# GpSimd forms W0's low part after VectorE's first one-hots, sums the bias on its own, and tile 1's registers are loaded earlier

## The reference

```python
h = jnp.maximum(_layernorm(x), 0.0)
# first layer: attention over the edges
h = nodes @ W + b_w                      # nodes is the h above; W is 512 x 512
s_dst, s_src = h @ a[:512], h @ a[512:]
e = leaky_relu(s_dst[dst] + s_src[src] + b_a, 0.2)
w = exp(e); alpha = w / segment_sum(w, dst)[dst]
out = segment_sum(alpha[:, None] * h[src], dst)
# x = x + out; then a second layer: gates over 4 experts, the best two taken,
# each two graph convolutions with 512 x 512 weights
```

## Time and profile before

| | us |
|---|---|
| median of 3 runs | 743.95 |
| the profiled execution | 743.08 |
| its span in the trace | 741.3 |
| TensorE busy | 720.8 (97%) |
| VectorE busy | 425.9 (57%) |
| ScalarE busy | 397.9 (54%) |
| GpSimd busy | 191.0 (26%) |

### The profile page before, as it was taken

The page is one execution under the profiler, slowest core; times in us unless marked ns, Lnnn a source line. Parts: engine busy times, 40 slices in busy tenths (PEclk is TensorE's granted clock), DMA queues, the critical chain, the costliest instruction groups (busy, mean ns, idle before and its releaser), DMA issues.

```text
span 741.3 us, 12237 instructions
## 1 busy us (share of the span) xinstructions
PE 720.8 (97%) x3671; PEld 586.5 (79%) x3671; DVE 425.9 (57%) x1053; ACT 397.9 (54%) x897; POOL 191.0 (26%) x207
## 2 busy tenths in 40 slices
PE   7899999999999999999999999999999999999994
PEld 5698977888888888777777777878888888888883
DVE  7989889999752538622722622657443544444441
ACT  8856678676643521511511511347677667767751
POOL 4300000000000101850200010045656555655511
PEclk9999999999999999999999999999999999999998
DMA  9100001111501247799699695379834994438950
GB/s 210 38 4 3 4 3 27 43 35 36 168 6 58 85 126 240 217 326 337 230 350 328 200 359 191 99 198 285 277 81 89 263 346 119 86 68 221 294 157 7
DMA packets 46445, 115.21 MB, mean 155 GB/s; under 512 B 8340, under 2 KB 8552, under 8 KB 46361
## 3 DMA queue, kind: packets, MB, share of 16 engines
q1 hardware_dynamic: 28581, 77.60, 32.5%
q0 software_dynamic: 9136, 19.65, 11.7%
q10 hardware_dynamic: 8644, 16.86, 7.0%
HBM read 64.89 MB, written 50.08 MB: 155 GB/s over the span
## 4 chain that ended last, share of the span: by engine, by line
PE 89%; DVE 6%; ACT 2%; issue 2%; DVEq 0%; POOL 0%; ACTq 0%; POOLq 0%
PE ps L1794 16%; PE ps L1795 16%; PE ps L1796 16%; PE ps L2223 7%; PE ps L2222 6%; PE ps L2090 3%; PE ps L2091 3%; PE ps L2023 3%; PE ps L2017 3%; PE ps L2018 3%; DVE onehot_g L1307 3%; PE ps L1882 2%; PE ps L2153 2%; PE ps L1961 1%; PE ps L1994 1%
## 5 line engine op out<-in xcount | busy, mean ns | idle before, releaser
L1121 ACT ACTIVATE agn<-ps,rec 32x128 f32<-32x128 f32 x336 | 120.9, 360 | 39.1 <-PE ps L2223 35.1
L1055 ACT ACTIVATE slots<-he_t 125x512 fp32r<-125x512 f32 x40 | 25.4, 635 | 150.9 <-DVE he_t L1592 144.5
L2223 PE MATMUL ps<-slots,CTs 125*128 x230 | 89.9, 391 | 0.0
L1592 DVE TENSOR_TENSOR he_t<-ps,b_b 125x512 f32<-125x512 f32 x40 | 27.5, 691 | 105.7 <-PE ps L1796 72.6
L734 POOL DMA_INDIRECT hrow<-t_d,piece_i x80 | 76.3, 954 | 25.7 <-issue 24.1
L2222 PE MATMUL ps<-slots,CTs 125*128 x207 | 80.7, 390 | 0.0
L1757 DVE TENSOR_TENSOR tm<-ps,b_b 128x512 f32<-128x512 f32 x23 | 15.9, 691 | 83.9 <-PE ps L1796 83.9
L1794 PE MATMUL ps<-W,agT_hi 128*125 128x512 f32 x160 | 63.5, 397 | 0.0
L1794 PE MATMUL ps<-W,h2T_hi 128*125 128x512 f32 x160 | 63.4, 396 | 0.0
L1796 PE MATMUL ps<-W,agT_lo 128*125 128x512 f32 x160 | 63.3, 396 | 0.0
L1795 PE MATMUL ps<-W,agT_hi 128*125 128x512 f32 x160 | 63.2, 395 | 0.0
(11 more groups left out here) (327 smaller groups left out, 1679.0 us busy)
## 6 DMA issues: line engine op xcount, KB each, us to landing
he_d<-slots SPq DMA_DIRECT2D x30, 448.0 KB
slots<-he_d SPq DMA_DIRECT2D x30, 448.0 KB
w_d<-slots SPq DMA_DIRECT2D x3, 4096.0 KB, 18.6
slots<-w_d SPq DMA_DIRECT2D x24, 512.0 KB, 21.8
t_d<-he_t SPq DMA_DIRECT2D x40, 224.0 KB
raw<-in_L_gnn_Wl ACTq DMA_DIRECT2D x4, 1024.0 KB, 8.0
raw<-in_L_gnn_Wr ACTq DMA_DIRECT2D x4, 1024.0 KB, 5.6
slots<-in_L_gnn_Wl ACTq DMA_DIRECT2D x4, 1024.0 KB, 10.3
```

The costliest lines, as they stand in the source:

```text
L1121: last = a.activation(agn[32 * r:32 * r + 32, q, :], ps[n, 3 + i % 2, 128 * r:128 * r + 128], ACT.Copy, scale=rec[n, i, 4:5])
L2223: last = mm(o, CTs[:, t, :], part(k, P, t * 1024 + D, P), start=False, stop=t == T - 1)
```

## The change

On GpSimd, the product of the bias with `a_sum` and its sum over the row are now made with tensor_tensor operations (a multiply, nine halvings, an add of `b_a`), around W0_hi; W0_lo waits in addition for the fifth `step_ready`, the last one-hot of VectorE's tile 0. On VectorE `bias_source` is gone, and the registers of tile 1 are loaded inside `sources()`, between the products and the wait for the last of them.

```diff
-            g.tensor_tensor(a_sum[:], a_b[0:P, 0, :], a_b[0:P, 1, :], ALU.add).then_inc(ab_ready.sem, 1)
+            link(g.tensor_tensor(a_sum[:], a_b[0:P, 0, :], a_b[0:P, 1, :], ALU.add))
+            link(g.tensor_tensor(a_sum[:], a_sum[:], bw_b[:], ALU.mult))
             pool.wait_ge(*w0_in(16))
             g.tensor_copy(W0_hi[:], W0_f[:]).then_inc(w0_hi_ready.sem, 1)
+            n = D // 2
+            while n > 0:
+                link(g.tensor_tensor(a_sum[:, 0:n], a_sum[:, 0:n], a_sum[:, n:2 * n], ALU.add))
+                n //= 2
+            g.tensor_tensor(s_add[:], a_sum[:, 0:1], ba_c[:], ALU.add).then_inc(ab_ready.sem, 1)
             pool.wait_ge(*w0_hi_ready(1))
+            pool.wait_ge(*step_ready(BW))
             g.tensor_tensor(W0_lo[:], W0_f[:], f32(W0_hi[:]), ALU.subtract).then_inc(w0_lo_ready.sem, 1)
...
             def sources():
                 source_vectors(1)
+                flags = batch_flags(1)
                 dve.wait_ge(*wa_f_ready(2 * KC))
                 link(v.tensor_copy(wa[:, :, 0:2], wa_f[:]))
                 v.tensor_tensor(wa[:, :, 2:4], wa_f[:], f32(wa[:, :, 0:2]), ALU.subtract).then_inc(wa_ready.sem, 1)
-
-            def bias_source():
-                dve.wait_ge(*ab_ready(1))
-                v.scalar_tensor_tensor(a_sum[:], bw_b[:], 1.0, a_sum[:], ALU.mult, ALU.mult,
-                                       accum_out=ab[:, 0:1]).then_inc(ab_ready.sem, 1)
-                dve.wait_ge(*ab_ready(2))
-                v.tensor_scalar(s_add[:], ab[:, 0:1], ba_c[:], None, ALU.add).then_inc(wa_ready.sem, 1)
+                return flags
...
-                more, before = batch_flags(b) if b > 0 else first_flags
+                more, before = (first_flags, *second_flags)[b] if b < 2 else batch_flags(b)
...
                 if b == 0:
-                    sources()
-                if b == 2:
-                    bias_source()
+                    second_flags.append(sources())
                 if b == T - 1:
...
-                    dve.wait_ge(*wa_ready(2))
+                    dve.wait_ge(*ab_ready(1))
```

More of the change, by code:

```diff
@@ L1361, in spread_out @@
                                 ).then_inc(sd_ready.sem, 1)
+            second_flags = []
             for b in range(T):
```

## The result

| | before | after |
|---|---|---|
| median of 9 runs, us | 744.10 | 747.93 |
| lowest and highest | 743.65 to 745.34 | 746.09 to 753.37 |
| profiled execution, its span | 743.08, 741.3 | 747.93, 746.2 |

The ratio is 1.0062, with a 95% interval of 1.0047 to 1.0077. Forecast were 744.1 us, no change, and a range up to 745.0: the measured median lies outside, on the slow side. The runs also lie further apart than before.

A forecast was written before the change was run, and what follows sets the result against it. TensorE, busy 97% of the span, was taken as the bound, so front delays pass through. +1.0 us at tile 1 and -0.81 at tile 3 gave +0.2 and 744.1 us, no change; range 741.4 to 745.0.

The forecast's parts named there:

- The mechanism: W0_lo enters after VectorE's first source product and holds the second some 4.4 us; TensorE waits for hT_lo and wa; chance 0.52.
- the first rival: VectorE's products run free beside W0_lo; -2.3 us, 741.65 us, faster; chance 0.26.
- the second rival: W0_lo gets in only at hT_lo or behind product 8; 743.55 or 744.7 us, no change; chance 0.12 for both forms.
- rival 3: Bias adds delay VectorE's first one-hots by 1.3 to 1.9 us, on top of the blocked products; 745.7 us, slower; chance 0.10.
- the two rules weighed: GpSimd blocked against VectorE's two-port modes only, or also operations with two SBUF inputs against a GpSimd operation reading SBUF.
- The step of tile 3: Without bias_source and its stall on VectorE, TensorE's tile-3 step falls from 7.61 to 6.80 us: -0.81 us.
- The sum: +1.0 us for TensorE late at tile 1, -0.81 at tile 3: +0.2 us.
- The prediction is wrong if the granted clock falls in TensorE's two new gaps: Stated sign of failure, without a size; the clock had stayed 1.00 from 20 to 33 us with 3 us idle.
- The start of tile 1: TensorE's tile 1 transposes start at 42.45 instead of 41.46 us: +1.0, bounds +0.7 to +1.9.
- The multiply was not hidden: Forecast that GpSimd's bias multiply, 1.27 us from 18.9 to 20.2, is hidden before W0_hi, which waits until 21.39.
- The scores behind a wait: TensorE's scores wait for wa until 41.65 and take 0.80 us before tile 1's transposes at 42.45.
- The moved loads: Some 1.2 of 1.6 us of VectorE's tile 1 register loads go; earns nothing itself, keeps the loss at 1.0.

The follow-up runs named there:

- E2: Changed kernel with W0_lo filled with zeros by a GpSimd memset in place of the subtraction: 740.72 us, ratio 0.9973 to the kernel before.
- E4: Changed kernel with W0_lo back directly behind W0_hi without its wait, the halvings and last add behind it: 741.96 us, ratio 0.9992 to the kernel before.
- E3: Kernel before with only W0_lo's added wait for the fifth step_ready: 745.5 us, ratio 1.0046.
- E11: Changed kernel with only the bias multiply moved behind W0_hi: 746.41 us, ratio 1.0028 to the kernel before.
- E1: Changed kernel with 15 filler matmuls before TensorE's wait for hT_lo and 7 before the first scores: 743.75 us, ratio 1.0014 to the kernel before.
- E9: The kernel with 15 and 7 filler matmuls in TensorE's gaps again, on the third chip: 745.61 us, ratio 1.0025 to the kernel before.
- E6: Changed kernel with W0_lo back behind W0_hi, epsilon added in ScalarE's root, scales before one-hots, bias adds after tile 3: 742.17 us, ratio 0.997 to before.
- E12: Changed kernel with W0_lo back, epsilon in ScalarE's root, scales before one-hots, bias adds and multiply held until tile 3 is done: 742.6 us, 0.9982 to before.
- E7: Changed kernel with tile 1's registers loaded at the head of tile 1 again: 746.75 us, ratio 1.0033 to the kernel before.
- E8: Changed kernel unaltered, run once more on the second chip: a single execution, 750.21 us.

## Why the prediction was wrong

**The mechanism was right.** W0_lo behind the first product, the second held until it is through, two waits of TensorE, the first rival's free products nowhere, the second rival's other turns nowhere, and rival 3's bias adds almost without cost. With W0_lo's reading taken away the kernel was 2.0 us faster than before (E2), with its old place given back 0.8 (E4); the new wait alone lost 2.7 (E3). Of the two rules weighed (the first names two-port modes, and doesn't exclude the rest), that of the Trainium skill's page SBUF — State Buffer (Who interferes with whom) held: the product with two SBUF inputs was held for 5.00 us by the operation that reads SBUF, and not at all by one that only writes. The memset is also another operation and a shorter one; no run changes the reading alone. The step of tile 3 gave back the 0.81 us forecast in every kernel in which `bias_source` was moved.

**The step that failed is the clock.** The sum had no term for it. It stood only as a last sentence, "The prediction is wrong if the granted clock falls in TensorE's two new gaps", and was put aside because the clock had stayed 1.00 from 20 to 33 us with 3 us idle. In the trace shown the fall cost 1.63 us in tile 1. From 33 to 66 us the clock fell in all four traces of the changed kernel and in E11. It did not fall there in E1 and E9, where fillers stand in the gaps, nor in E2, E4, E6 and E12, which have no such gaps. It cost 1.6 us where it reached tile 1, and 0.1 where it was over before.

What isn't settled is when it falls. E3 and E7 have the same gaps and kept 1.00 in the one execution of each that was traced (the slowest of E3, 748.04 us, had a mean clock of 0.992 over the span, and wasn't traced). The kernel before, too, waits 1.61 us and then 0.43, 1.0 us apart, ahead of 30.6 us, and kept 1.00:

```profile
29.14 0.53 PE L1805 MATMUL ps<-onehot_p 125*125 125x250 bf16 x3 [1.61 <-ACT onehot_p L800]
30.55 0.54 PE L1805 MATMUL ps<-onehot_p 125*125 125x250 bf16 x3 [0.43 <-ACT onehot_p L800]
```

In E6 and E9 it fell from 14 us on, with TensorE busy. The gaps made a fall likely; they don't fix it.

**The clock isn't all of it.** The median moved by 3.8 us: 0.2 forecast, 1.6 the clock, 0.8 a later start of tile 1, and some 1.2 that came behind the front. Where the clock stayed 1.00 in the traced front, the kernel still lost 1.0 and 1.5 us (E1, E9), a little more than the 0.9 that the stated range allowed. The start of tile 1 was 1.76 us late where the sum had 1.0, and within the bounds of +0.7 to +1.9 given for it; its 0.77 us too much have the two sources that follow.

**The multiply was not hidden.** The prediction placed it "in front of W0_hi, which waits for W until 21.39: hidden". That names what waits behind it on GpSimd, and not what VectorE does beside it. There `tab_b`, ten elements, is held until the multiply ends: 0.54 us for 0.15 in the trace shown, 1.21 in E8. Everything behind it on VectorE, the statistics and `std`, is late by as much; `std` starts at 26.06 instead of 25.7. How much it is depends on when the small loads land: the add that precedes the multiply starts between 17.14 and 18.47 us in these traces. The last one-hot came at 31.5 instead of 31.2, and the other stations kept that 0.3: hT_lo ends at 38.95 against 38.65, the scores start at 41.95 against 41.65.

**The scores behind a wait were 0.47 us too short.** They were put at 0.80 us, from the earlier trace rows, where `wa` had long been there. Behind the wait the way to the transposes takes 43.22 - 41.95 = 1.27, of which 0.27 is issue. 0.3 and 0.47 are the 0.77 by which tile 1's start, 42.45, was missed.

**Two slips in the working** changed nothing. Its bounds for tile 1, less 0.81, give -0.1 to +1.1 us, not the -0.3 and +0.9 from which the range was made. And at 25.7 us four of the ten adds are still to come, by its own lengths and in the trace, not "some six".

**The moved loads** were said to earn nothing of their own but to keep the loss at 1.0. The loads took 0.94 us less (0.69 for 1.63), and without them in their new place the front loses 0.77 more (E7 and E3).

**What stays open**, beside the clock, is the late part. In the kernels with the clock at 1.00 from 33 to 66 us the time moved by up to 0.6 us more than the front. In the changed kernel some 1.2 us are left over, and single executions are far longer (up to 753.37). A wait of 0.6 to 1.4 us for `hT_f` at about 490 us stood in every trace of the second and third chip and in that shown of the changed kernel, the faster E6 and E12 among them (0.6 and 1.3 us), but in none of the first chip nor in that of the kernel before. So it isn't the work of the change alone; no run here separates its cause.

## What to carry to other kernels

Moving a long operation off one victim of a lock moves the lock: look at what the other engine runs at the new place, and at every small operation with its operands in SBUF beside each new GpSimd operation, not only at what waits behind it. A new gap in TensorE's work can be paid twice, once as idle time and once for the clock in the work behind it; give the second a term of its own in the sum. Keep the gap from arising if you can; filler matmuls kept the clock up here (E1, E9), but those kernels were still slower than before. Where one small operation is held, it is cheaper to let another engine do it (E6) than to move the long one.

## What the runs showed of the hardware

- A GpSimd tensor_tensor with two SBUF inputs got in at the first boundary between two VectorE products of two SBUF inputs, and held the second until it was through (W0_lo ended at 36.58 us, the product at 37.12): 5.00 to 5.02 us instead of 0.69 in the nine traces with that pair. A memset of the same 128x2048 beside it took 1.81 us and held nothing (0.68).
- A small VectorE operation can be held too: `tab_b` with 1x10 elements took up to 1.21 us instead of 0.15, `std` with 125x10 2.23 instead of 0.21, `shift` with 125x10 and two SBUF inputs 0.89 instead of 0.17. Not all are: the reciprocal of 125x10 beside the same W0_lo took 0.22 (E12), two casts from PSUM beside the multiply 0.19 and 0.16, and operations of one element (`fl_f`, `flag_i`, in E1) 0.13 to 0.14.
- Gaps of 1.4 to 1.8 us, in part with a second of 0.8, were followed by half clock in five of the seven traces that have them, in one and the same kernel now from 38.7 us on and now from 44. Two gaps of 0.9 and 0.6 us in E9 were too. Gaps of 1.61 and 0.43 us before the change were not, and in E6 and E9 the clock fell at 14 us with TensorE busy.
- Matmuls behind a wait start later than their own length says: eight scores and the step to the next block took 1.27 us, against 0.80 when their operands were early.
